# Sums of two states' products by accumulating DMAs in place of additions on POOL

## The reference

```python
xz = x @ w_in.T + b_in
x_ssm, z = jnp.split(xz, 2, axis=-1)
z = jax.nn.silu(z)
dt = jax.nn.softplus(x_ssm @ w_dt.T + b_dt)
Bm = x_ssm @ w_B.T + b_B
Cm = x_ssm @ w_C.T + b_C
def step(h, inp):                       # h: (B, 512, 16)
    xt, dtt, bt, ct = inp
    dA = jnp.exp(A[None] * dtt[..., None])
    dB = dtt[..., None] * bt[:, None, :]
    h = dA * h + dB * xt[..., None]
    y = jnp.sum(h * ct[:, None, :], axis=-1)
    return (h, y)
y = (y + D * x_ssm) * z
y = y @ w_out.T + b_out
```

## Time and profile before

| | |
|---|---|
| median of the timed runs | 4589.9 us (2 runs, 4588.63 to 4591.16) |
| span of the profiled execution | 4588.9 us |
| PE matmul busy | 4344.2 us, 95% |
| POOL busy | 4161.1 us, 91% |
| ACT busy | 3817.6 us, 83% |
| DVE busy | 3679.8 us, 80% |
| additions of products on POOL (L375) | 512 of 1276 ns, 653.4 us |

### The profile page before, as it was taken

The page is one execution under the profiler, slowest core; times in us unless marked ns, Lnnn a source line. Parts: engine busy times, 40 slices in busy tenths (PEclk is TensorE's granted clock), DMA queues, the critical chain, the costliest instruction groups (busy, mean ns, idle before and its releaser), DMA issues. The chain is left out here.

```text
span 4588.9 us, 71982 instructions
## 1 busy us (share of the span) xinstructions
PE 4344.2 (95%) x22528; PEld 2805.6 (61%) x22528; DVE 3679.8 (80%) x5132; ACT 3817.6 (83%) x6371; POOL 4161.1 (91%) x3343
## 2 busy tenths in 40 slices
PE   7999999999999999999999999999999999999997
PEld 3666666666666666666666666666666666666664
DVE  3778888888887888888888888888878888888885
ACT  3788888888888888888888888888888888888885
POOL 3899999999999999999999999999999999999995
PEclk8999999999999999999999999999999999999999
DMA  3111111111111111111121111111111111111111
GB/s 129 45 43 58 58 58 45 56 51 57 60 58 48 49 59 59 58 46 54 51 62 59 59 44 56 51 57 60 54 45 54 60 61 58 47 53 51 58 49 39
DMA packets 140915, 254.79 MB, mean 56 GB/s; under 512 B 18597, under 2 KB 18597, under 8 KB 140538
## 3 DMA queue, kind: packets, MB, share of 16 engines
q1 hardware_dynamic: 140538, 250.19, 17.2%
HBM read 215.50 MB, written 34.63 MB: 55 GB/s over the span
## 5 line engine op out<-in xcount | busy, mean ns | idle before, releaser
L364 POOL TENSOR_TENSOR work<-work,c_bc 128x512 f32<-128x512 f32 x2048 | 2590.8, 1280 | 266.6 <-DVE work L1127 180.9
L1127 DVE TENSOR_TENSOR_SCAN work<-work,state,b_ps 128x512 f32<-128x512 f32 x1792 | 2250.5, 1273 | 351.9 <-PE b_ps L453 343.2
L839 ACT ACTIVATE work<-u_td,b_td 128x512 f32<-128x512 f32 x2048 | 1455.4, 711 | 147.5 <-PE b_ps L453 142.2
L829 ACT ACTIVATE work<-dt_t,neg_a 128x512 f32<-128x512 f32 x2048 | 1454.1, 710 | 12.5 <-DVE work L1127 12.1
L453 PE MATMUL b_ps<-ident,work 128*128 128x128 f32 x8192 | 1246.2, 275 | 67.2 <-DVE work L1127 57.0
L453 PEld LDWEIGHTS b_ps<-ident,work 128*128 128x128 f32 x8192 | 966.7, 142 | 344.5 <-issue 173.4
L530 PEld LDWEIGHTS y_ps<-ident,work 128*128 128x128 f32 x6144 | 758.4, 142 | 635.7 <-issue 586.5
L530 PE MATMUL y_ps<-ident,work 128*128 128x128 f32 x6144 | 916.2, 274 | 4.7 <-POOL work L375 3.5
L375 POOL TENSOR_TENSOR work<-work 128x512 f32<-128x512 f32 x512 | 653.4, 1276 | 40.2
L679 PE MATMUL dense<-h_t,w_in_t 128*128 128x512 f32 x1024 | 514.4, 599 | 9.2 <-DVE u_td L1210 8.9
L587 PE MATMUL dense<-w_out_t,proj 128*128 128x512 f32 x1024 | 508.6, 594 | 0.0
(11 more groups left out here) (115 smaller groups left out, 4523.0 us busy)
## 6 DMA issues: line engine op xcount, KB each, us to landing
c_bc<-c_d SPq DMA_DIRECT2D x512, 256.0 KB, 3.2
xn<-in_x SPq DMA_DIRECT2D x128, 256.0 KB, 5.1
x<-in_x SPq DMA_DIRECT2D x128, 256.0 KB, 4.4
out_dram<-x SPq DMA_DIRECT2D x128, 256.0 KB, 4.2
work<-in_wmod SPq DMA_DIRECT2D x2, 1024.0 KB, 6.3
w_in_t<-in_w_in_t SPq DMA_DIRECT2D x2, 1024.0 KB, 9.9
gain_shift<-par_d SPq DMA_DIRECT2D x8, 256.0 KB, 4.5
w_dt_t<-in_w_dt_t SPq DMA_DIRECT2D x1, 1024.0 KB, 11.3
```

What stands on the lines that cost most here:

```text
L364: gp.tensor_tensor(pr[:, (s * U + i) % PR_RING, :], hs[:, (s * U + i) % HS_RING, :], c_bc[:, (s * N + n) % C_RING, :], ALU.mult).then_inc( ...
L829: A(decay[:, (s * U + i) % DEC_RING, :], dt_t[:, s % 2, j, :], ACT.Exp, scale=neg_a[:, j, n:n + 1]).then_inc(S["dec_done"], 1)
L839: A(v[:, n % V_RING, tb, :], u_td[:, tb, :], ACT.Copy, scale=b_td[:, s % 2, tb, n:n + 1]).then_inc(S["v_done"], 1)
L1127: V.tensor_tensor_scan(hs[:, (s * U + i) % HS_RING, :], decay[:, (s * U + i) % DEC_RING, :], b_ps[:, i % 2, :], state[:, i:i + 1] if s % N ...
```

## The change

Each of the 512 additions of L375 becomes a DMA that POOL issues: from the held product's buffer to the newer product's, both in SBUF, with the sum as the operation of the write (`accum_op`). The order of instructions on POOL is the same otherwise. The semaphore `sum_done` goes; in its place there are four, `sum_landed[j]`, one for each channel block, and each DMA raises its own by 16 once its data has landed. Between two DMAs with the same semaphore lie at least four units. `landed(k, i)` is the count that stands for a DMA of unit i in chunk k. PE's `add_unit` and POOL's product wait on it.

```diff
-    def sums(i):
-
-        return sum(summed(r // KD) for r in range(i + 1))
+    def landed(k, i):
+
+        return Q * (k * len(HELD) + sum(summed(n) for n in range(i // KD + 1)))
...
                 if r // KD in HELD:
-                    gp.wait_ge(S["sum_done"], at("sum_done", k, sums(r + KD)))
+                    if k >= 0:
+                        gp.wait_ge(sum_landed[r % KD], landed(k, r + KD))
...
             def add_products(s, i):
 
                 gp.wait_ge(S["prod_done"], at("prod_done", s, i + 1))
-                gp.tensor_tensor(pr[:, (s * U + i) % PR_RING, :], pr[:, (s * U + i) % PR_RING, :],
-                                 pr[:, (s * U + i - KD) % PR_RING, :], ALU.add).then_inc(S["sum_done"], 1)
+                gp.dma_start(pr[:, (s * U + i) % PR_RING, :], pr[:, (s * U + i - KD) % PR_RING, :],
+                             accum_op=ALU.add).then_inc(sum_landed[i % KD], Q)
...
                 if summed(i // KD):
-                    pe.wait_ge(S["sum_done"], at("sum_done", s, sums(i)))
+                    pe.wait_ge(sum_landed[j], landed(s, i))
```

More of the change, by code:

```diff
@@ L177, in build_program @@
             "SP": dict(stored_0=Q, stored_1=Q, stored_2=Q, stored_3=Q, c_stored=Q),
-            "Pool": dict(prod_done=U, skip_added=KD, sum_done=sums(U - 1), xsh_done=TB, x1_done=TB, dt_done=KD, u_done=KD, sz_done=KD),
+            "Pool": dict(prod_done=U, skip_added=KD, xsh_done=TB, x1_done=TB, dt_done=KD, u_done=KD, sz_done=KD),
             "PE": dict(b_made=U, y_added=added(U - 1), s_ps=1, g_used=J, yz_ps=KD, out_ps=TB, res_used=TB, pre_ps=TB, xt_ps=KD, xs_ps=KD,
@@ L191, in build_program @@
         S = {n: ctx.enter_context(nc.semaphore(n)) for n in once + list(COUNT)}
-        x_loaded, xb_loaded, c_loaded, wm_loaded = (
+        x_loaded, xb_loaded, c_loaded, wm_loaded, sum_landed = (
             [ctx.enter_context(nc.semaphore(f"{n}_{m}")) for m in range(count)]
-            for n, count in (("x_loaded", TB), ("xb_loaded", TB), ("c_loaded", C_RING), ("wm_loaded", 6)))
+            for n, count in (("x_loaded", TB), ("xb_loaded", TB), ("c_loaded", C_RING), ("wm_loaded", 6), ("sum_landed", KD)))
         def at(name, k, n):
```

## The result

The changed kernel takes 4731.2 us (median of 2 runs, 4725.42 to 4736.96) against 4589.9 us: a ratio of 1.0309 [1.0278, 1.034], so it is 3.1% slower.

A forecast was written before the change was run, and what follows sets the result against it. PE was taken to bound the kernel; terms for unit 39, unit 59 and the gate made 0.92 us a stage, times 32 stages 29 us: 4588.9 + 29 + 1.0 = 4619 us. The range was 4545 to 4840 us.

The forecast's parts named there:

- What bounds the kernel: In the scan stages PE is the bound, busy 133.6 of 139.3 us; POOL is a close second at 129.8.
- rival A: At the sums and gate: all transfers hidden and the gate earlier, 4563 us, at most down to 4522; chance 0.20.
- c: Time that one DMA issue holds POOL: taken as 1.3 us, with bounds of 0.320 and 2.5 us.
- rival B: On POOL: an issue holds it longer than an addition and it becomes the bound, 4778 us; chance 0.27.
- The gate's term: At unit 6's gate on POOL: three issues ahead of it make it later by 0.06 us a stage.
- T: From the start of POOL's issue until PE may use the sum: 4.9 us, between 3.2 and 7.3.
- Unit 39's term: At PE's use of unit 39's sum: seven issues ahead and a late landing cost 0.41 us a stage.
- its term of 0.45 us: At PE's use of unit 59's sum: three issues ahead and a late landing cost 0.45 us a stage.
- No queue is near full: DMA engines are 17 to 18% busy; the 512 transfers add 16% of the run.
- The clock has no part in this: On PE the granted clock is 1.00 throughout (2.4 GHz), so the forecast has no term for it.
- Nothing hides PE's wait: At PE's add_unit, a wait for a sum holds the queued turn_v and the next scan, so it counts in full.
- Rival C: At the landing of sums: issues are short but DMA engines add more slowly than they copy, 4738 us; chance 0.20.

The follow-up runs named there:

- e9: The kernel before (additions on POOL) with the last channel block's gate at POOL's position 5 in place of 6: 4521.4 us, 0.9851.
- e5: The changed kernel with three matmuls of zeros on PE where it stands still before the sum of unit 59: 4696.3 us, 1.023.
- e1: The changed kernel with SP issuing the next x loads only after the sum of unit 59 has landed: 4606.5 us, 1.0034.
- e10: The changed kernel with x loads held until unit 59's sum has landed and the gate at position 5 in place of 6: 4576.5 us, 0.9968.
- e7: The changed kernel with one DMA for two units, a ring of 10 products, smaller DMA scratch, x loads after the last pair has landed: 4641.9 us, 1.0113.
- e14: The changed kernel with one of four x loads issued at once, three after unit 59's sum has landed: 4643.2 us, 1.0116.

## Why the prediction came out as it did

- **What bounds the kernel**: right. PE is the bound, and the gate's lateness was worth 68 us as the prediction's upper bound for rival A had it (4522 us; e9 gives 4521.4). That the two agree to a microsecond is chance: the bound took DVE's wait of 2.13 us a stage, and a stage became 2.5 us shorter; PE's own wait at L566 was 1.5 us.
- **c, POOL's time per issue**: the block itself is 0.877 us where 1.3 was taken, inside the bounds. But it isn't all. Ahead of it stands a gap of 0.30 us in place of 0.08, and the product that starts 0.61 us after the issue's start takes 1.58 us instead of 1.28; the issue is not one block of time, which the prediction had named as a sign of being wrong. From sum to next sum within a block it is 2.49 us against 2.59: POOL gets 0.10 us back a sum, not the 0.40 that c = 0.88 would give. An issue thus weighs as much as an addition of 1.18 us, under the 1.43 from which rival B decides. The gate's term had the wrong sign but the right smallness: it comes 0.3 us sooner, and the wait shrinks by 7.0 us in the run instead of growing by 2.
- **T, one landing time for all sums**: this is the step that failed. Taken was 4.9 us for each. It is 3.3 us for an undisturbed sum and 4.5 us for the fourth of a block, both in time in most stages. Unit 39's term of 0.41 us a stage isn't there in 23 of 32 stages; in the other nine it is 10.5 us in all, not far from the 13 us of the forecast, but for reasons that the sum didn't have: loads beside it, and a deadline of 3.2 to 3.4 us that was read in stage 14 only, as 4.63. For unit 59 T is 7.15 us, and its term of 0.45 us is 2.75 us: from unit 58's scan to unit 59's matmuls 13.89 us (median), against 11.14 before. T depends on what SP issues within a microsecond of it.
- **"No queue is near full"**: it rested on the mean share of 17 to 18%; the 16% that the DMAs were to add came as 16.4. At the one place that decides, the share is 0.90 for 4 us. The trace of before had it to see: in it SP issues the four x loads 0.32 us after unit 59's addition starts (2164.07 against 2163.75, in the first rows of stage 14 above).
- **"The clock has no part in this"**: true of the kernel before, not of the changed one. It costs 35 us by e5, up to 50 by the page, and the sum had no term for what a new standstill does to the clock.
- **Nothing hides PE's wait**: right; 2.75 us a stage over 30 stages are 83 us, and with the clock's 35 to 50 us that makes 118 to 133 us; e1, which takes away both, gave back 125. The first stage's 7 us come on top.
- **Rival C** (slow landing, since the engines add slowly): half right. Adding doubles the packets' time, and a landing past 5.9 us decides, which is what happened, at one sum of sixteen. The price was of its size, 4738 us, for another reason: it had four small terms, and there was one large one and the clock. That 4738 is near the 4731 measured is luck.

In sum, the direction and the range held, and the size didn't: +29 us was forecast and +141 came, from a term that should have been read at its own place. The first stage's share is located beside the gain and shift loads, but no run moved these. Why the sum's packets stay out of the engines for 2 us once SP's have begun stays open; the runs show only which issues bring it on.

## What to carry to other kernels

Before an instruction becomes a DMA, list for each place in the loop what the other queues issue from a microsecond before to a microsecond after it: a DMA that lands in 3.3 us alone took 7 us where two loads were issued next to it, and a mean share of the DMA engines doesn't tell this. Read the deadlines in more than one stage, too: unit 39's was 4.63 us in one and 3.23 us in another. If a stall of the bounding matrix engine follows, add the time that the slower clock takes after it. And a wait that another engine's order causes may be had for one line: moving the gate was worth ten times what the DMAs could give.

## What the runs showed of the hardware

- The first packet of a POOL DMA came 1.45 us after its issue started (1.15 us for a plain copy), that of an SP load 0.96 us after. Four x loads that SP issued from 0.10 us after POOL's DMA on held it off for 2.2 us more (1.45 to 3.69 us). One store issued 0.09 us after it (e10) moved its first packet to 2.34 us.
- An accumulating DMA within SBUF took 187 ns for 2 KB against 160 to 170 ns for a copy's 4 KB, and 343 ns for 4 KB in pairs (e7); its issue took 0.88 us against 0.58.
- POOL's issue cost 0.88 us for 256 KB and for 512 KB alike, and the product behind it took 1.58 us instead of 1.28 (of a plain copy: 1.28).
- PE stood still for 2.5 us (median) at unit 59, and the granted clock fell to the lower level for 95.6 us in 24 stretches, 4.0 us each; with 1.2 us (e14) it mostly did not (3 stretches in the run).
